# Adjacency of a sparse graph from two small one-hots per edge block and 16 destinations, with fp32 edge weights, in place of one large one-hot per edge block and 32 destinations

## The reference, cut to what matters

```python
x = x + gnn0(layernorm(x), edge_index)        # agg = segment_sum(x[src], dst), then two batch-normed products
x = x + ffn0(layernorm(x))                    # eight experts, routed by sinkhorn
x = x + gnn1(layernorm(x), edge_weight)       # agg = segment_sum(x[dst] * edge_weight, src), one product
x = x + ffn1(layernorm(x))                    # a tree of eight leaves, 512 -> 2048 -> 512 each
```

## Time and profile before

| | us |
|---|---|
| median of 3 runs | 2289.66 |
| span of the profiled execution, first to last instruction | 2288.6 |
| what the median has over the span | 1.06 |
| phase_edges, to VectorE's last instruction | 28.7 |
| phase_adjacency, first instruction to POOL's last | 30.3 to 184.8 |
| TensorE, VectorE, ScalarE, POOL busy in the whole | 2170.6, 1587.2, 1067.9, 621.4 |

### The profile page before, as it was taken

The page is one execution under the profiler, slowest core; times in us unless marked ns, Lnnn a source line. Parts: engine busy times, 40 slices in busy tenths (PEclk is TensorE's granted clock), DMA queues, the critical chain, the costliest instruction groups (busy, mean ns, idle before and its releaser), DMA issues.

```text
span 2288.6 us, 32781 instructions
## 1 busy us (share of the span) xinstructions
PE 2170.6 (95%) x11859; PEld 1904.1 (83%) x11859; DVE 1587.2 (69%) x2606; ACT 1067.9 (47%) x1857; POOL 621.4 (27%) x1066
## 2 busy tenths in 40 slices
PE   5898998588999999999999999999999999999999
PEld 4887996457858888888888888888888888888888
DVE  8994356636477767777777677777776777777765
ACT  4335235345365445455554445555544455555443
POOL 1453000111112332233223322332233223322320
PEclk9998998598999999999999999999999999999999
DMA  2000202251001111111111111111111111111111
GB/s 72 3 2 1 74 1 76 70 167 37 28 23 46 47 42 38 43 50 42 37 49 49 38 38 49 48 38 38 55 43 37 38 58 40 37 38 60 38 38 55
DMA packets 71028, 101.99 MB, mean 45 GB/s; under 512 B 5847, under 2 KB 41255, under 8 KB 70871
## 3 DMA queue, kind: packets, MB, share of 16 engines
q1 hardware_dynamic: 67523, 94.20, 13.0%
q0 software_dynamic: 3040, 5.19, 0.8%
q10 hardware_dynamic: 308, 0.51, 0.1%
HBM read 92.14 MB, written 7.74 MB: 44 GB/s over the span
## 4 chain that ended last, share of the span: by engine, by line
PE 73%; issue 0%; ACT 0%; DVE 0%
PE psum L550 24%; PE psum L551 24%; PE psum L552 24%; PE psum L2143 1%; PE psum L2036 0%; PE psum L2026 0%; ACT w_forms_hi L1878 0%; PE psum L2043 0%; DVE x_rows L2290 0%; ACT f_rows L544 0%; DVE x_rows L2322 0%; DVE stats L508 0%; DVE hidden L2207 0%; ACT w_forms_hi L1876 0%; ACT w_forms_hi L1874 0%
## 5 line engine op out<-in xcount | busy, mean ns | idle before, releaser
L550 PE MATMUL psum<-w_hi,hidden_hi 128*125 128x512 f32 x1280 | 504.0, 394 | 2.4 <-issue 2.4
L551 PE MATMUL psum<-w_lo,hidden_hi 128*125 128x512 f32 x1280 | 505.1, 395 | 0.0
L552 PE MATMUL psum<-w_hi,hidden_lo 128*125 128x512 f32 x1280 | 505.0, 395 | 0.0
L551 PE MATMUL psum<-x_forms_lo,w_forms_hi 128*128 128x418 f32 x1260 | 445.5, 354 | 0.0
L1819 POOL TENSOR_TENSOR w_forms<-w_raw 128x128 f32<-128x128 f32 x189 | 104.9, 582 | 1128.5 <-PE psum L552 586.2
L2290 DVE SCALAR_TENSOR_TENSOR x_rows<-psum,leaf_by_token,x_rows 125x512 f32<-125x512 f32 x320 | 233.9, 748 | 255.2 <-PE psum L552 255.2
L1916 ACT ACTIVATE hidden<-psum 128x418 f32<-128x418 f32 x315 | 161.7, 513 | 488.2 <-PE psum L552 486.0
L550 PEld LDWEIGHTS psum<-w_hi,hidden_hi 128*125 128x125 f32 x1280 | 237.8, 186 | 58.8 <-issue 2.7
L552 PEld LDWEIGHTS psum<-w_hi,hidden_lo 128*125 128x125 f32 x1280 | 237.2, 185 | 59.1
L551 PEld LDWEIGHTS psum<-w_lo,hidden_hi 128*125 128x125 f32 x1280 | 237.5, 186 | 54.3
L2263 DVE TENSOR_TENSOR hidden_lo<-hidden,hidden_hi 128x418 fp32r<-128x418 f32 (+1 forms) x384 | 254.8, 689 | 21.7 <-ACT hidden_hi L1938 21.7
(11 more groups left out here) (354 smaller groups left out, 3528.7 us busy)
## 6 DMA issues: line engine op xcount, KB each, us to landing
w_raw<-in_w SPq DMA_DIRECT2D x127, 512.0 KB, 3.7
expert_raw<-in_experts SPq DMA_DIRECT2D x8, 1024.0 KB, 5.6
expert_results_d<-expert_results SPq DMA_DIRECT2D x16, 160.0 KB, 4.6
c_rows_d<-c_rows SPq DMA_DIRECT2D x10, 250.0 KB
x_rows<-in_x SPq DMA_DIRECT2D x5, 448.0 KB
W_raw<-in_gnn_W SPq DMA_DIRECT2D x4, 512.0 KB, 4.1
W_raw<-in_gnn_W SPq DMA_DIRECT2D x1, 2048.0 KB, 9.6
b_by_token<-in_b SPq DMA_DIRECT2D x8, 256.0 KB, 3.7
```

What stands on the lines that cost most here:

```text
L550: t.matmul(out, stat[0], mov[0], start=start, stop=False, skip_group_check=again)
L551: t.matmul(out, stat[0], mov[1], start=False, stop=False, skip_group_check=again)
L552: return t.matmul(out, stat[1], mov[0], start=False, stop=stop, skip_group_check=again)
```

## The change

Windows have 16 destinations, 81 of them, of which three make a set, so 27 sets. Per pair of window and edge block there are now two small fp32 one-hots, of a column number (ten source tiles x 16 destinations, 160 columns) and of the source within its tile (128 columns). A count matmul multiplies them as bf16 (the upper halves of their fp32 words), a weight matmul multiplies the source one-hot times weight by the column one-hot in fp32. A window takes three blocks; further ones are taken by the set, in a loop. The weight is no longer cut. VectorE makes the one-hots by three pairs in one instruction; ScalarE multiplies the source one-hot by the weight and drains both matrices straight into A0T and A1T; POOL has no part. The setup picks key, source and weight of the 243 pairs with matmuls by a one-hot of block numbers. The loads are in another order, dst first. Cut to its core:

```diff
-WIN = 32
-NW = -(-N // WIN)
-SLOTS = 4
-KEY = 2048
+WIN = 16
+SET = 3
+NSETS = -(-N // (SET * WIN))
+NW = NSETS * SET
+SLOTS = 3
+SET_PAIRS = SET * SLOTS
+COLUMNS = NT * WIN
+KEY = 256
...
 def phase_edges(nc, sem, g):
...
         @block.sync
         def _(sp):
-            for to, of in loads:
-                sp.dma_start(to, of).then_inc(loaded, 16)
-            sp.dma_start(i10f[:, :], g.consts_d[:, C_I10:C_Q]).then_inc(i10_loaded, 16)
+            sp.dma_start(raw_i[:, 1, :], g.dst.rearrange("(q e) -> q e", q=EQ)).then_inc(dst_loaded, 16)
+            sp.dma_start(g.small[:, :], g.consts_d[:, 0:C_SMALL]).then_inc(small_loaded, 16)
+            sp.dma_start(raw_i[:, 0, :], g.src.rearrange("(q e) -> q e", q=EQ)).then_inc(src_loaded, 16)
+            sp.dma_start(g.edge_consts[:, :], g.consts_d[:, C_COL:C_Q]).then_inc(tables_loaded, 16)
+            sp.dma_start(wraw[:, :], g.edge_weight.rearrange("(q e) -> q e", q=EQ)).then_inc(w_loaded, 16)
...
         @block.vector
+            v.wait_ge(dst_loaded, 16)
+            s.then(v.tensor_single_scalar(win_i[:, :], raw_i[:, 1, :], 4, ALU.logical_shift_right))
...
+            v.wait_ge(src_loaded, 16)
+            s.then(v.tensor_scalar(scaled_i[:, :], raw_i[:, 0, :], float(SRC_MUL), float(16 << SRC_SHIFT),
+                                   ALU.mult, ALU.add))
...
+            at.diag = s.mark(v.tensor_scalar(diag[:, :], g.ident[0:NW, 0:NW], lohi[:, 0:1], None, ALU.mult))
...
+            v.wait_ge(firsts_spread, 1)
+            shape = [EQ, 2 * SLOTS, NW]
+            at.chosen = s.mark(v.tensor_tensor(
+                chosen[:, :, :, :].rearrange("q h u w -> q (h u) w"),
+                g.psum[0:EQ, 2, 0:NW].unsqueeze(1).to_broadcast(shape),
+                g.slot_at[0:EQ, :].unsqueeze(2).to_broadcast(shape), ALU.is_equal))
...
         @block.tensor
+            for a, of in enumerate(rows):
+                for h in range(2):
+                    ins = t.matmul(picked(a), of[:, h * EB:(h + 1) * EB],
+                                   chosen[:, h, :, :].rearrange("q u w -> q (u w)"), start=h == 0, stop=h == 1)
+                ins.then_inc(pairs_picked, 1)
...
 def phase_adjacency(nc, sem, g):
+    RING = 3
...
         @block.vector
+            for n in range(NSETS):
+                if n >= RING:
+                    v.wait_ge(used, n - RING + 1)
+                for j in range(SET):
+                    at = slice(j * SLOTS, (j + 1) * SLOTS)
+                    shape = [EB, SLOTS, 128]
+                    v.tensor_tensor(L[:, n % RING, at], g.lows[0:EB, :].unsqueeze(1).to_broadcast(shape),
+                                    g.pair_low[:, n * SET + j, :].unsqueeze(2).to_broadcast(shape),
+                                    ALU.is_equal).then_inc(low_made, 1)
+                    shape = [EB, SLOTS, COLUMNS]
+                    v.tensor_tensor(E[:, n % RING, at], g.columns[0:EB, :].unsqueeze(1).to_broadcast(shape),
+                                    g.pair_key[:, n * SET + j, :].unsqueeze(2).to_broadcast(shape),
+                                    ALU.is_equal).then_inc(column_made, 1)
+                with v.Fori(0, extra[n % LOAD]) as k:
...
         @block.tensor
+                t.wait_ge(drained, 2 * (n + 1))
+                for j in range(SET):
+                    t.wait_ge(low_made, n * SET + j + 1)
+                    t.wait_ge(column_made, n * SET + j + 1)
+                    for u in range(SLOTS):
+                        q = j * SLOTS + u
+                        t.matmul(piece(n, 0, j), ones_of(L[:, n % RING, q, :]), ones_of(E[:, n % RING, q, :]),
+                                 start=q == 0, stop=False, skip_group_check=True)
+                for j in range(SET):
+                    t.wait_ge(weighted, SET_PAIRS * n + SLOTS * (j + 1))
+                    for u in range(SLOTS):
+                        q = j * SLOTS + u
+                        ins = t.matmul(piece(n, 1, j), LW[:, n % RING, q, :], E[:, n % RING, q, :],
+                                       start=q == 0, stop=False, skip_group_check=True)
+                ins.then_inc(used, 1)
...
         @block.scalar
+            def drain(n):
+                a.wait_ge(summed, n + 1)
+                for which, to in ((0, g.A0T), (1, g.A1T)):
+                    a.activation(to[:, :, n * SET * WIN:n * SET * WIN + wide].rearrange("p c (w d) -> p c w d", d=WIN),
+                                 bank(n, which).rearrange("p (w c d) -> p c w d", w=SET, c=NT)[:, :, 0:windows, :],
+                                 ACT.Copy).then_inc(drained, 1)
+            for n in range(NSETS):
+                if n >= RING:
+                    a.wait_ge(used, n - RING + 1)
+                for q in range(SET_PAIRS):
+                    w, u = n * SET + q // SLOTS, q % SLOTS
+                    if u == 0:
+                        a.wait_ge(low_made, w + 1)
+                    a.activation(LW[:, n % RING, q, :], L[:, n % RING, q, :], ACT.Copy,
+                                 scale=g.pair_w[:, w, u:u + 1]).then_inc(weighted, 1)
...
+                if n >= 1:
+                    drain(n - 1)
+            drain(NSETS - 1)
-        @block.gpsimd
...
```

More of the change, by code:

```diff
@@ L199, in phase_edges @@
     lohi = room("lohi", [NW, 2], F32)
[L200 to L203, removed]
+    span = room("span", [NW, 1], F32)
+    diag = room("first_diag", [NW, NW], F32)
+    chosen = room("slot_onehot", [EQ, 2, SLOTS, NW], F32)
+    most = room("most_extra", [1, NSETS], F32)
     at = Record()
[L206 to L209, removed]
-    later_loaded = sem("e_later_loaded")
[L211 to L217, removed]
+    dst_loaded = sem("e_dst_loaded")
+    src_loaded = sem("e_src_loaded")
+    w_loaded = sem("e_w_loaded")
+    small_loaded = sem("e_small_loaded")
+    tables_loaded = sem("e_tables_loaded")
+    later_loaded = sem("e_later_loaded")
+    extents_turned = sem("e_extents_turned")
+    blocks_turned = sem("e_blocks_turned")
+    firsts_spread = sem("e_firsts_spread")
+    pairs_picked = sem("e_pairs_picked")
+    rows_turned = sem("e_rows_turned")
+    vecs_turned = sem("e_vecs_turned")
+    pairs_copied = sem("e_pairs_copied")
     later_loads = [
@@ L231, in phase_edges, with picked @@
     ]
-    shape = [EB, NB, WIN]
+    def picked(which):
+        bank = (4, 5, 7)[which]
+        return g.psum[0:EB, bank, 0:SLOTS * NW]
     with nc.Block() as block:
@@ L290, in _ @@
             s.then(v.tensor_reduce(ends[:, 1:2], pick[:, 1, :], X, ALU.max))
[L291 to L306, removed]
@@ new lines, in _ @@
+            v.wait_ge(firsts_spread, 1)
[4 more added lines that the diff above has]
+                g.slot_at[0:EQ, :].unsqueeze(2).to_broadcast(shape), ALU.is_equal))
+            v.wait_ge(blocks_turned, 1)
+            table = g.psum[0:EB, 0, 0:6 * EQ].rearrange("p (a h q) -> p a q h", a=3, h=2)
+            for a in range(3):
+                s.mark(v.tensor_copy(halves(g.by_block[:, a, 0:NB]), table[:, a]))
@@ new lines, in _ @@
+            v.wait_ge(pairs_picked, 1)
+            s.mark(v.tensor_tensor(g.pair_key[:, :, :].rearrange("p w u -> p u w"),
+                                   picked(0).rearrange("p (u w) -> p u w", u=SLOTS),
+                                   g.w2k[0:EB, :].unsqueeze(1).to_broadcast([EB, SLOTS, NW]), ALU.subtract))
+            v.wait_ge(rows_turned, 1)
+            s.mark(v.tensor_copy(g.firsts[:, :], g.psum[0:1, 6, 0:NW]))
+            s.then(v.tensor_reduce(most[:, :], g.psum[0:1, 6, NW:2 * NW].rearrange("o (g j) -> o g j", j=SET),
+                                   X, ALU.max))
@@ L309, in _ @@
+            s.mark(v.tensor_single_scalar(g.extra[:, :], most[:, :], 0.0, ALU.max))
+            v.wait_ge(vecs_turned, 1)
             s.mark(v.tensor_copy(g.vecs[:, :], g.psum[:, 3, 0:96]))
-            s.mark(v.tensor_copy(g.b1cols[:, :], g.psum[:, 3, 128:256]))
+            s.then(v.tensor_copy(g.b1cols[:, :], g.psum[:, 3, 128:256]))
         @block.scalar
         def _(a):
-            a.wait_ge(g.steps.semaphore, at.rem)
-            a.activation(rem16[:, :, :], rem[:, :].unsqueeze(2).to_broadcast(shape), ACT.Copy).then_inc(rem_spread, 1)
@@ L316, in _ @@
[L316 to L319, removed]
+            for c, to in ((1, g.pair_low), (2, g.pair_w)):
+                a.wait_ge(pairs_picked, c + 1)
+                a.activation(to[:, :, :].rearrange("p w u -> p u w"), picked(c).rearrange("p (u w) -> p u w", u=SLOTS),
+                             ACT.Copy).then_inc(pairs_copied, 1)
@@ L321, in _ @@
+            a.wait_ge(pairs_copied, 2)
         @block.tensor
         def _(t):
-            t.wait_ge(loaded, 16 * len(loads))
+            t.wait_ge(g.steps.semaphore, at.spread)
+            for a in range(4):
+                ins = t.matmul(g.psum[0:NW, 1, a * EQ:(a + 1) * EQ], spread[:, a, :], g.ident[0:EQ, 0:EQ],
+                               start=True, stop=True)
+            ins.then_inc(extents_turned, 1)
+            t.wait_ge(w_loaded, 16)
```

(95 more changed lines are left out.)

185 lines of the change are left out of this document (71 added, 114 removed).

## The result

The changed kernel takes 2274.24 us (median of 4 runs, 2274.10 to 2275.63), the kernel before 2289.39 in the same measurement; the ratio is 0.9936, 95% interval 0.9922 to 0.9950. So it is faster by 15 us, or 0.6%, where 50 us were forecast. The profiled execution took 2274.19 us, its span is 2272.4.

What follows compares the result with a forecast made beforehand. TensorE was taken to set the adjacency stage's pace, ScalarE and VectorE close behind. Setup gain 11.2 us and a 116 us stage put the next block at 135.4 instead of 185.15, gain 49.7: 2240 us, range 2224 to 2262.

Steps and rivals of the forecast that it cites:

- Setup: Edge setup before the adjacency stage: the stage's first instruction at 19.1 us instead of 30.32, gain 11.2, bounds 8.5 and 13.
- the slot one-hot: In the setup: one-hot of 486 elements read from PSUM, 0.51 + 0.16 us, done at 11.5.
- the twelve picking records: In the setup: twelve fp32 TensorE passes of 243 columns that pick the pairs, taken as 4.2 us, to 15.7.
- the change of block: Between the setup's end on VectorE and the adjacency stage's first instruction: 1.6 us, as before.
- Durations: Adjacency stage, per instruction: one-hots 0.47 and 0.57 us, counts 0.074, weight records about 0.14, ScalarE's copies 0.385, starts 0.285 apart.
- The rule of 81 ns a matmul: TensorE's counts in the stage: the skill's figure, not adopted, would add 20 ns each, 5 us, forecast 2245.
- The count of extra rounds: Adjacency stage: about five sets with a fourth block, 5.3 us on TensorE; on VectorE 2.5 each, 12 us.
- Rival 4: Adjacency stage: half of the sets have a fourth block, nine more rounds at 2.5 to 3.5 us, 2265; chance 0.04.
- The sum: Adjacency stage, engine loads: TensorE 110, ScalarE 100, VectorE 102 us; with lead, filling and low clock the stage takes 116.
- Rival 1: Adjacency stage: ScalarE and handoffs bound, 0.385 us a copy makes ScalarE 125, stage 128, time 2252; chance 0.20.
- Rival 2: Adjacency stage: TensorE lighter than thought, VectorE and ScalarE at 102 bound, setup 1 us better, 2228; chance 0.08.
- Rival 3: Adjacency stage: TensorE's short waits keep its clock at 1.2 GHz, stage 198 us, time 2322, slower; chance 0.06.

Runs made afterwards that it cites:

- skipping kernel: The changed kernel with the loop of extra rounds entered, on VectorE and TensorE, only where the set's count is not zero; 2237.61 us.
- the last run: The kernel before, with the loop left out of windows 10 and 39, which have nothing left to loop over; 2289.10 us, ratio 1.0002.
- the plain copies: The skipping kernel with ScalarE's 243 copies at a constant scale of 1 instead of one read from SBUF; 2237.66 us.
- the run with two rounds: The changed kernel with every set's count of extra rounds raised to at least 2, matrices unchanged; 2433.27 us.
- TensorE alone skips: The changed kernel with VectorE making every round, TensorE only handing the buffers back where the count is zero; 2268.72 us.

## Why the prediction was wrong

**Setup: right, in part by luck.** 19.1 forecast, 19.09 measured. The pieces were off both ways: the slot one-hot starts at 9.9 instead of 10.8 since dst was there by 2.7 us and not 3.9; the twelve picking records then take 5.2 us (10.62 to 15.84), not 4.2; VectorE ends at 17.1 instead of 17.5; and the change of block is 2.0 us instead of 1.6.

**Durations: right.** VectorE's one-hots start 0.47 and 0.57 us apart, as forecast (62.59, 63.06, and the next at 63.63). In the skipping kernel's trace nine count matmuls in a row take 0.81 us, the last one 0.24 of it, so 0.072 each against 0.074; that their bf16 operands are read every second one cost nothing. Eighteen weight records take 2.65 with the last one's 0.31, so 0.138 against 0.142. ScalarE's copies are 0.40 long against 0.385, and nine in a row take 2.73 us, so 0.29 apart against 0.285. The rule of 81 ns a matmul from the Trainium skill (TensorE: Matmul & The Clock Gate, Back-to-back issue gap) is not borne out in these runs either: 0.072 for 160 columns.

**The count of extra rounds: the step that failed.** "From the inputs I count about five sets with one": the inputs do give four, but the kernel makes 27 rounds, as the loop runs its body before it tests its count. VectorE's 102 became 144, TensorE's 110 became 140, and VectorE in place of TensorE the bound. With that term mended, 27 rounds in place of five, and at the 2.0 us that a round takes instead of 2.5, the forecast's own sum for VectorE is 90 + 54 = 144, as measured. The row that told it was in my hands: the earlier trace rows has L401 44 times where the same count over windows of 32 gives 42; the other two were windows with nothing to loop over, as the last run shows. Rival 4 had the mechanism's place, extra rounds that don't go, but with half the sets and 4% of the chance. Its price was off too: 25 us for nine rounds would be 61 for 22, about 2301, since it puts every round on top of TensorE's sum, where the 23 empty ones measured 36.6 us. That the changed kernel is faster at all, the forecast's 0.92, rests on the setup: the stage as it ran gave about 4 us.

**The sum: right to a few us once the empty rounds are out.** The skipping kernel is what the forecast thought it forecast: 2240 against 2237.61, TensorE 108.6 busy against 110, VectorE 99 against 102, ScalarE 102 against 100. The next block comes at 131.85 against 135.4: 1.4 of these 3.5 us are TensorE's own sum, the rest is in the 6 us that the forecast put on top of it for ScalarE's lead, the filling and the low clock.

**Rival 1** (ScalarE and handoffs) is refuted by the plain copies; its 0.385 us a copy was 0.29. **Rival 2** (a lighter TensorE) did not come; TensorE was only 1.4 us below its sum. **Rival 3** (the low clock) did not come in the changed kernel, clock 0.99, but the run with two rounds shows that the low clock can come in this stage: 0.70 from 100 to 150 us, with TensorE idle for 9.9 of the 50. What makes it fall these runs don't tell: where TensorE alone skips it is idle for 27 of 142.9 us, and the clock stays at 0.99.

## What to carry to other kernels

When a change moves work into a loop whose count is read at run time, find out what the loop does at a count of zero; where the body runs once all the same, a path that is nearly always empty is paid every time, here 37 of the 51 us that were to be had. Check each instruction count of the trace against the count that the data should give, and don't pass over a difference of two in 44. And look at the engine that makes the operands: taking the empty rounds from TensorE alone gave 5.5 us, taking them from VectorE as well gave the other 31.

## What the runs showed that I had not expected

A second round per set cost 5.9 us where an empty first one cost 1.6 ((2274.24 - 2237.61)/23), for the same instructions: a single set of buffers is free when the first round comes and makes the engines take turns in the second, and the low clock comes on top. Neither a test and branch for 23 sets on two engines (0.7 us in all) nor reading every second bf16 in both operands of a matmul (0.072 us for 160 columns) cost anything that could be measured.
